# A transformer layer on eight cores: a reordered head, evened head pairs, and wider rows of values

## The chip, the cores and the metric

The kernel runs on the eight cores of one Trainium2 chip. Each core takes one of the eight sequences of the batch and works alone; all cores hold a copy of the weights. The metric is the device time in microseconds of the slowest core.

## The reference

For one sequence x of 2048 rows and 1024 columns:

```
xn  = layernorm(x)
q, k, v = xn Wq, xn Wk, xn Wv            (16 heads of 64 columns)
out = softmax(q k^T / 8) v               (per head)
x1  = x + xn + out Wp
h   = layernorm(x1) W1 W2 W3             (three 1024 x 1024 weights)
y   = x1 + tanh(h + bias)
```

The kernel folds W1 W2 W3 into one matrix on the chip (the "folds"), since nothing nonlinear stands between them.

## The kernel before

There are five engines with a queue of instructions each: TensorE (matmuls and transposes), ScalarE, VectorE, GpSimd and SyncE. All waits are written out by hand: `need(engine, token)` makes an engine wait for a semaphore, and an engine works through its instructions in the order in which the Python code emits them. Where a function is called therefore decides what stands behind what.

**The head** (lines 555 to 677). The 16 tiles of x, 128 rows each, are loaded by SyncE (L172). For each tile VectorE makes the statistics (`ln1_stats`: bn_stats L559, bn_aggr L561) and adds epsilon (L567), GpSimd raises to the power -1/2 (L569) and forms minus mean times that (`nm`, L575). The normalised tile `xn` is written by GpSimd (L579), every fourth by ScalarE (`ln1_se`, L584). Tiles 0 and 1 go singly; from tile 2 on, `ln1_power` serves two tiles at once, so that it waits for the statistics of both. TensorE transposes each tile in eight pieces (`ln1_turn`, L604), and ScalarE copies the result into `S` (L610). Once four tiles are in `S`, a group g of 512 rows can be projected: `first_proj` runs eight matmuls of 512 columns for q or k (`proj_mms`, L217) or 32 of 128 columns for v (`v_mms`, L256). Weight slices of one head pair are loaded by GpSimd's queue (`load_slice`, L178), each with a cast from float to bfloat16 (512 KB read, 256 KB written); the first, wk of pair 0, is issued before the memsets that fill both buffers of v with ones (L187). In the loop of L619, group g's k and q projections follow the transposes of its own tiles, and its v projection stands before the transposes of the next group's last two tiles. After the loop come k and q of group 3, two k groups of pair 1 (`unit_k`, L646 and L658), the squares of q and k (`square`, L234, on VectorE), and the guard: three small steps (`guard1` to `guard3`, L289, L302, L311) that turn the largest squared norms into one constant `cb`, which every exponential of the pair subtracts. `guard1` needs all squares of q and k. Between the guards TensorE does half of v's last group.

**The loop** (L760) goes over 8 pairs of heads, in each over 8 chunks of 256 query rows, and in each over 8 units of two key tiles. `emit_qk` makes scores for both heads (L370), `emit_exp` one exponential of 128 x 1024 (L382), `emit_pv` eight matmuls (L398): the probabilities are the weights, and 65 columns of v are the moving operand: 64 values of one head of one key tile and a column of ones, which gives the row sum. Such a row of v lies in SBUF at a stride of VW = 66 elements of 2 bytes, 132 bytes. The results of a chunk stand in one PSUM bank, again at a stride of 66 (there of 4 bytes). `emit_norm` divides by the sums, `turn_ao` transposes.

Between these, TensorE has filler units: projections of the next pair (`unit_k`, `unit_q`, `unit_v`), and the folds (`unit_w12`, `unit_w123`), 32 in all, spread over pairs 0 to 6 by `N_FOLD`. `queue_pair` lists the units of a pair. A chunk has two regular places for a unit; what a pair has over 16 (`extra`) is put in by an additional `advance(8)` and `finish()` in chunk 1 or 3, after step 1. The listed units before are 16 in pairs 0 to 4 and 6, and 17 in pair 5. All of them share one PSUM bank, so that a unit starts only when the eviction of the one before, by VectorE, is done. The last fold of W1 W2 starts the load of W3, and it stands first in pair 3.

**The tail** adds x1, the output projection, the second normalisation and the folded matrix, row tile by row tile.

Of the kernel before, what the change touches and what calls it, by code (L numbers as in the profile page):

```python
# [9 lines left out]
F32 = mybir.dt.float32  # L10
# [7 lines left out]
NT = N // 128  # L18
NK = D // 128
NP = 8  # L20
EPS = 1e-5
VW = 66

QC = 256
NSLOT = 3
# [26 lines left out]
def build_program():  # L52
# [14 lines left out]
    with ctx:  # L67
        def sb(name, cols, dt):
            return E(nc.sbuf_tensor(name, [128, cols], dt))
# [17 lines left out]
        onesb = sb("onesb", 1, BF16)  # L87
        sixteenth = sb("sixteenth", 128, F32)
        biasb = sb("biasb", D, F32)
        mhalf = sb("mhalf", 2, F32)  # L90
        st6 = [sb(f"st6_{i}", 12, F32) for i in range(4)]
        mv = sb("mv", 2 * NT, F32)
        ve = sb("ve", NT, F32)
        rs = sb("rs", NT, F32)
        rs1 = sb("rs1", NT, F32)
        nm = sb("nm", NT, F32)
        mv2 = sb("mv2", 2 * NT, F32)
        ve2 = sb("ve2", NT, F32)
        rs2 = sb("rs2", NT, F32)
# [77 lines left out]
        def load_slice(n, p):  # L177
            return d_w[n][p % 2].inc(GP.dma_start(wsl[n][p % 2][:], wqkv_d[n, p]))  # L178

        w_in = {(1, 0): load_slice(1, 0)}  # L180
        half_in = s_gp.inc(GP.memset(mhalf[:], -0.5))
        need(SE, half_in)
        s_se.inc(SE.activation(nm2[:, 0:1], mhalf[:, 0:1], AF.Identity))
# [202 lines left out]
        def emit_pv(t):  # L386
            p, c, u = iters[t]
            need(TE, exp_in[t])
            if u == 0:
                need(TE, bank_free[PV0])  # L390
            for i in range(MPI):
                m = MPI * u + i
                need(TE, v_in[(p, m // 4)])
                for qt in range(NQT):
                    for h in range(2):
                        col = VW * (qt * 2 + h)
                        off = 512 * h + QC * i + 128 * qt
                        ins = TE.matmul(bank[PV0][:, col:col + 65],  # L398
                                        P[t % NPB][:, off:off + 128],
                                        v[p % 2][:, VW * (2 * m + h):VW * (2 * m + h) + 65],  # L400
                                        start=(u == 0 and i == 0 and qt == 0 and h == 0),
                                        stop=(u == NU - 1 and i == MPI - 1), skip_group_check=True)
            pv_mm[t] = s_te.inc(ins)
            pv_done[p] = pv_mm[t]

        def emit_norm(p, c):

            i = (p * NCQ + c) % 2
            nb = 2 * NQT
            need(VE, pv_done[p], norm_in.get((p * NCQ + c) - 2))  # L410
            sums = bank[PV0][:, 0:VW * nb].rearrange("p (g c) -> p g c", c=VW)
            m = s_ve.inc(VE.reciprocal(rc[i][:], sums[:, :, 64]))
            need(VE, m, ao_mm.get((p * NCQ + c) - 2))
            norm_in[p * NCQ + c] = bank_free[PV0] = s_ve.inc(VE.tensor_tensor(  # L414
                ao[i][:].rearrange("p (g c) -> p g c", c=64), sums[:, :, 0:64],
                rc[i][:].unsqueeze(2).to_broadcast([128, nb, 64]), ALU.mult))
# [135 lines left out]

        xn1 = [xn[i] if i < NXN else P[i - NXN] for i in range(2 * NXN)]

        def ln1_stats(t):
            need(VE, x_in[t])
            st = st6[t % 4]
            for h in range(2):
                m = s_ve.inc(VE.bn_stats(st[:, 6 * h:6 * (h + 1)], x_tile[t][:, 512 * h:512 * (h + 1)]))  # L559
            need(VE, m)  # L560
            return s_ve.inc(VE.bn_aggr(mv[:, 2 * t:2 * t + 2], st[:]))  # L561

        def ln1_power(t, n, m):

            var = mv[:, 2 * t:2 * (t + n)].rearrange("p (t c) -> p t c", c=2)[:, :, 1]
            need(VE, m)
            m = s_ve.inc(VE.tensor_scalar(ve[:, t:t + n], var, EPS, None, ALU.add))  # L567
            need(GP, m, gp_ones)
            m = s_gp.inc(GP.tensor_tensor(rs[:, t:t + n], ve[:, t:t + n], mhalf[:, 0:n], ALU.pow))  # L569
            need(GP, m)  # L570

        nm_in = {}

        def ln1_gp(t):
            nm_in[t] = m = s_gp.inc(GP.tensor_scalar(nm[:, t:t + 1], mv[:, 2 * t:2 * t + 1], rs[:, t:t + 1],  # L575
                                                     -1.0, ALU.mult, ALU.mult))
            if t % 4 != 0:
                need(GP, m, t1_mm.get(t - 2 * NXN))
                xn_in[t] = s_gp.inc(GP.tensor_scalar(xn1[t % (2 * NXN)][:], x_tile[t], rs[:, t:t + 1],  # L579
                                                     nm[:, t:t + 1], ALU.mult, ALU.add))  # L580
# [6 lines left out]
        def ln1_pair(j):

            if j == 0:
                ln1_power(0, 1, ln1_stats(0))  # L590
                ln1_gp(0)
                ln1_power(1, 1, ln1_stats(1))
                ln1_gp(1)
                return
            ln1_stats(2 * j)
            ln1_power(2 * j, 2, ln1_stats(2 * j + 1))
            ln1_gp(2 * j)
            ln1_gp(2 * j + 1)

        def ln1_turn(t, eng, sem):  # L600
            b = next_bank()
# [8 lines left out]
            bank_free[b] = sem.inc(SE.copy(dst, src) if eng is SE else VE.tensor_copy(dst, src))  # L610
            S_in[t // 4].append(bank_free[b])

        def first_proj(n, g):

            b = next_bank()
            run(v_mms(0, g, b) if n == 2 else proj_mms(n, 0, g, b))
            return b

        for j in range(NT // 2 + 1):  # L619
            g = j // 2 - 1  # L620
            if j < NT // 2:
                ln1_pair(j)
            if j == 0:
                w_in[(0, 0)] = load_slice(0, 0)
            if j == 1:
                w_in[(2, 0)] = load_slice(2, 0)
            if j == 5:
                w_in[(1, 1)] = load_slice(1, 1)
            if j % 2 and g >= 0:
                evict_qk(0, 0, g, held[0], SE, s_se)  # L630
            if j > 0:
                ln1_turn(2 * j - 2, SE, s_se)
                last = (VE, s_ve) if 2 * j == NT else (SE, s_se)
                ln1_turn(2 * j - 1, *last)
            if j < NT // 2 and j % 2 == 0:
                ln1_se(2 * j)
            if g >= 0 and j < NT // 2:
                if j % 2 == 0:
                    held = {1: first_proj(1, g), 0: first_proj(0, g)}
                    evict_qk(1, 0, g, held[1], SE, s_se)  # L640
                else:
                    held[2] = first_proj(2, g)
                    evict_v(0, g, held[2], SE, s_se)


        run(unit_k(1, 0, squared=False))  # L646
        b = first_proj(1, 3)
        evict_qk(1, 0, 3, b, VE, s_ve)
        for g in range(3):
            square(1, 0, g)  # L650
            square(0, 0, g)
        square(1, 0, 3)
        b = first_proj(0, 3)
        evict_qk(0, 0, 3, b, SE, s_se)
        square(0, 0, 3)
        ring["banks"] = [4, 5, 6, 7]
        ring["i"] = 0
        run(unit_k(1, 1, squared=False))  # L658
        guard1(0, next_bank())()
        for t in range(BATCH):  # L660
            emit_qk(t)
        guard2(0, next_bank())()
        b = next_bank()
        values = v_mms(0, 3, b)
        for _ in range(16):
            next(values)
        guard3(0, next_bank())()
        run(values)
        evict_v(0, 3, b, VE, s_ve)
        for g in range(2):  # L670
            square(1, 1, g)
        need(GP, x_in[NT - 1])
        for n in (0, 2):
# [4 lines left out]

        need(VE, xn_in[NT - 2], xn_in[NT - 1])
        rs1_in = s_ve.inc(VE.tensor_scalar(rs1[:], rs[:], 1.0, None, ALU.add))
        ring["banks"] = [FL0]

# [188 lines left out]
```

How the kernel before makes its waits and increments, by code:

```python
    def inc(self, instr):  # L46
        instr.then_inc(self.h, self.step)
        self.n += self.step
        return (self, self.n)
# [2 lines left out]
def build_program():  # L52
# [106 lines left out]
        def need(eng, *tokens):  # L159
            for tok in tokens:
                if tok is None:
                    continue
                sem, n = tok
                if waited.get((eng, sem), 0) < n:
                    eng.wait_ge(sem.h, n)
                    waited[(eng, sem)] = n
# [652 lines left out]
        turn_ao(NP - 1, NCQ - 1, next_bank())()  # L820
        push_chunk(NCQ - 1)
        for t, fh in ((NT - 3, 0), (NT - 3, 1), (NT - 2, 0)):
            units.append(unit_ff(t, fh))
        units.append(unit_t2(NT - 1))
        for t, fh in ((NT - 2, 1), (NT - 1, 0), (NT - 1, 1)):
            units.append(unit_ff(t, fh))
        while units:
            run(units.popleft())
        for s in d_o:
            SP.wait_ge(s.h, s.n)
        nc.all_engine_barrier()
    return nc
```

## Time and profile before

| | us |
|---|---|
| median of 3 runs | 728.6 |
| lowest, highest | 728.41, 823.76 |
| profiled execution | 729.96 |
| its span, core 6 (the slowest) | 728.2 |
| spans of the other cores | 725.1 to 727.6 |
| TensorE, ScalarE, VectorE, GpSimd busy | 681.6, 599.4, 264.4, 125.3 |

The span is the time from the first to the last instruction of a core; the profiled execution's own time is a little longer. An engine's busy time counts the time in which at least one of its instructions was at work. Matmuls overlap in the pipeline, so a single one lasts longer in the records than the distance to the next; the chain of waits gives runs of matmuls by that distance. The highest of the three runs is far above the other two; the median is not moved by it.

### The profile page before, as it was taken

How to read it: one execution, taken by the hardware profiler on the slowest of the kernel's cores; microseconds unless marked ns; L12 is line 12 of the kernel's file. 1: busy time of each engine (PE TensorE's matmuls, PEld its weight loads, DVE VectorE, ACT ScalarE, POOL GpSimd, SP SyncE). 2: the span in 40 equal slices, each digit the busy share in tenths (PEclk: the TensorE clock that was granted, in tenths of full speed). 3: DMA queues.
4: the chain of work that ended last, by engine and by line, in shares of the span. 5: the costliest groups of instructions: out<-in, count | busy, mean ns of one | idle time of the engine just before them, and what ended most of it. 6: DMA issues, size and time to landing. Idle time of an engine off the chain costs nothing.

```text
span 728.2 us, 21958 instructions; the slowest of 8 cores (725.1 to 728.2 us)
## 1 busy us (share of the span) xinstructions
PE 681.6 (94%) x9112; PEld 432.3 (59%) x9112; DVE 264.4 (36%) x590; ACT 599.4 (82%) x600; POOL 125.3 (17%) x169
## 2 busy tenths in 40 slices
PE   1699999999999999999999999999999989999996
PEld 0465676667666765676667656665676555444443
DVE  4724322332223322322332233224322343556663
ACT  2566999999999999999999989999999899444443
POOL 5871000000000002000000000012010121366654
PEclk9999999999999999999999999999999999999999
DMA  8959700111010004610110000032024000334332
GB/s 229 283 72 166 135 9 3 16 16 16 4 16 2 2 3 69 107 17 2 17 22 12 16 2 3 2 88 88 2 41 80 1 3 2 109 124 155 134 116 116
DMA packets 13344, 41.87 MB, mean 57 GB/s; under 512 B 1600, under 2 KB 1728, under 8 KB 13248
## 3 DMA queue, kind: packets, MB, share of 16 engines
q0 software_dynamic: 5904, 15.21, 13.7%
q1 hardware_dynamic: 7056, 25.17, 10.4%
q8 instruction: 74, 1.21, 0.7%
q14 instruction: 22, 0.18, 0.1%
q10 hardware_dynamic: 288, 0.10, 0.1%
HBM read 46.76 MB, written 8.39 MB: 76 GB/s over the span
## 4 chain that ended last, share of the span: by engine, by line
PE 86%; DVE 4%; issue 3%; DMA 3%; ACT 3%; POOL 0%; DVEq 0%; SPq 0%; ACTq 0%; POOLq 0%
PE sc L370 18%; PE pv L398 16%; PE fl L217 14%; PE fl L256 8%; PE sc L521 5%; PE fl L343 4%; PE fl L326 4%; PE sc L464 4%; PE fl L464 3%; ACT P L382 2%; DMA aoT<-x 2%; PE fl L422 2%; PE sc L217 1%; DMA wv<-wqkv 1%; PE pv L521 1%
## 5 line engine op out<-in xcount | busy, mean ns | idle before, releaser
L382 ACT ACTIVATE P<-sc,cb 128x1024 bf16<-128x1024 f32 x512 | 528.3, 1114 | 36.4 <-PE sc L370 24.4
L398 PEld LDWEIGHTS pv<-v,P 128*128 128x128 bf16 x4096 | 157.7, 97 | 44.1 <-issue 17.2
L398 PE MATMUL pv<-v,P 128*128 128x65 bf16 x4096 | 173.5, 193 | 5.4 <-DVE ao L414 2.6
L370 PE MATMUL sc<-qT,kT 64*128 64x256 bf16 x2048 | 157.5, 272 | 1.8 <-ACT P L382 1.8
L370 PEld LDWEIGHTS sc<-qT,kT 64*128 64x128 bf16 x2048 | 78.5, 94 | 42.8 <-issue 25.2
L532 ACT ACTIVATE S<-S 128x512 f32<-128x512 f32 x32 | 20.1, 629 | 58.2 <-DVE S L528 58.2
L256 PE MATMUL fl<-wv,S 128*128 128x128 bf16 x960 | 63.6, 219 | 1.8 <-DVE aoT L429 0.4
L256 PEld LDWEIGHTS fl<-wv,S 128*128 128x128 bf16 x960 | 54.1, 98 | 12.4 <-issue 12.2
L217 PE MATMUL fl<-S,wq 128*128 128x512 bf16 x224 | 57.8, 380 | 0.5
L217 PE MATMUL fl<-S,wk 128*128 128x512 bf16 x208 | 53.5, 380 | 3.1 <-DVE ao L414 1.3
L268 DVE CAST v<-fl 128x512 bf16<-128x512 f32 x29 | 20.0, 691 | 78.8 <-PE fl L256 78.8
L521 PE MATMUL sc<-bufB,S 128*128 128x512 bf16 x192 | 45.0, 379 | 0.5 <-ACT S L514 0.5
L540 POOL TENSOR_TENSOR S<-S,xs 128x512 f32<-128x512 f32 x30 | 38.1, 1271 | 41.8 <-ACT S L532 41.8
L228 DVE CAST qT<-fl 128x512 bf16<-128x512 f32 x28 | 19.4, 691 | 71.1 <-PE fl L217 71.1
L228 DVE CAST kT<-fl 128x512 bf16<-128x512 f32 x26 | 18.0, 691 | 67.6 <-PE fl L217 67.6
L326 PE MATMUL fl<-bufA,bufB 128*128 128x512 bf16 x128 | 33.1, 380 | 1.1 <-DVE g L306 0.7
L343 PE MATMUL fl<-bufA,bufC 128*128 128x512 bf16 x128 | 33.1, 380 | 1.0 <-DVE g L306 0.8
L457 POOL TENSOR_SCALAR xs<-xs,rs,nm 128x1024 f32<-128x1024 f32 x16 | 19.2, 1202 | 75.1 <-DVE aoT L429 72.6
L464 PE MATMUL sc<-bufC,aoT 128*128 128x512 bf16 x136 | 32.1, 379 | 0.0
L521 PEld LDWEIGHTS sc<-bufB,S 128*128 128x128 bf16 x192 | 18.6, 98 | 22.6 <-issue 0.9
L217 PEld LDWEIGHTS fl<-S,wq 128*128 128x128 bf16 x224 | 17.5, 97 | 24.0 <-issue 9.8
L429 DVE COPY aoT<-fl 128x256 bf16<-128x256 bf16 x63 | 18.3, 291 | 35.7 <-PE fl L422 13.4
(128 smaller groups left out, 555.8 us busy)
## 6 DMA issues: line engine op xcount, KB each, us to landing
xs<-x SPq DMA_DIRECT2D x22, 512.0 KB, 6.0
out<-S SPq DMA_DIRECT2D x15, 512.0 KB, 2.9
aoT<-x SPq DMA_DIRECT2D x8, 512.0 KB, 12.7
wk<-wqkv POOLq DMA_DIRECT2D x8, 256.0 KB, 9.0
wq<-wqkv POOLq DMA_DIRECT2D x8, 256.0 KB, 4.9
wv<-wqkv POOLq DMA_DIRECT2D x8, 256.0 KB, 5.9
bufA<-w1t POOLq DMA_DIRECT2D x4, 512.0 KB, 14.3
bufB<-w POOLq DMA_DIRECT2D x4, 512.0 KB, 25.0
```

Source lines behind the costliest of these rows:

```text
L217: ins = TE.matmul(bank[b], wsl_k[n][p % 2][:, k, :], S_k[:, k, 512 * g:512 * (g + 1)], start=(k == 0), stop=(k == NK - 1))
L228: SE.copy(dst, bank[b]) if eng is SE else VE.tensor_copy(dst, bank[b]))
L256: ins = TE.matmul(bank[b][:, 128 * j:128 * (j + 1)], S_k[:, k, 128 * t:128 * (t + 1)], wsl_k[2][p % 2][:, k, :], start=(k == 0), stop=(k = ...
L326: ins = TE.matmul(bank[b], B_k[:, k, 128 * e:128 * (e + 1)], A_k[:, k, 512 * ch:512 * (ch + 1)], start=(k == 0), stop=(k == NK - 1))
L343: ins = TE.matmul(bank[b], C_k[:, k, 128 * ct:128 * (ct + 1)], A_k[:, k, 512 * fh:512 * (fh + 1)], start=(k == 0), stop=(k == NK - 1))
L370: ins = TE.matmul(sc[s][:, 512 * h + QC * i:512 * h + QC * (i + 1)], kT[p % 2][64 * h:64 * (h + 1), 128 * m:128 * (m + 1)], qT[p % 2][64 * ...
L382: exp_in[t] = s_se.inc(SE.activation(P[t % NPB][:], sc[s][:], AF.Exp, bias=cb[p % 2][:], scale=0.125))
L398: ins = TE.matmul(bank[PV0][:, col:col + 65], P[t % NPB][:, off:off + 128], v[p % 2][:, VW * (2 * m + h):VW * (2 * m + h) + 65], start=(u ...
L464: ins = TE.matmul(bank[b], ao_k[:, k, 128 * t:128 * (t + 1)], C_k[:, k, 512 * fh:512 * (fh + 1)], start=(k == 0), stop=(k == NK - 1))
L521: ins = TE.matmul(bank[b], xn2T[t % 3][:, k, :], B_k[:, k, 512 * fh:512 * (fh + 1)], start=(k == 0), stop=(k == NK - 1))
L532: m = s_se.inc(SE.activation(h, h, AF.Tanh))
L540: add_done[t] = s_gp.inc(GP.tensor_add(h, h, x1_tile(t)[:, 512 * fh:512 * (fh + 1)]))
```

## The change

1. The stride of a row of v goes from 66 to 96 elements (132 to 192 bytes). The stride in PSUM stays 66, now called PW. The two buffers of v grow from 4,224 to 6,144 bytes a partition each.
2. The head: each tile of x goes through its own statistics and power; VectorE also writes the negated mean (`ngm`), and GpSimd normalises as (x + ngm) x rs in one instruction, so that it needs no `nm` first. Only every fourth tile makes `nm` at once; VectorE makes the whole `nm` later, for the tail. Tile 15 is normalised by VectorE. wk of pair 0 is loaded when x0 is in. v of a group is projected after the transposes of the next group's tiles (g = 0) or among them. Three k groups of pair 1 are now projected in the head, the first two inside the loop over groups. Six of the eight squares move into the loop over groups. Eight v matmuls, not sixteen, stand between the second and third guard, and eight before the first.
3. `N_FOLD` goes from [7, 4, 4, 4, 4, 5, 4] to [8, 4, 4, 4, 4, 4, 4], and no fold is moved to the front of pair 3. Pair 0 lists one k projection fewer. Each of pairs 0 to 6 then lists 16 units.

```diff
-VW = 66
+VW = 96
+PW = 66
...
-        w_in = {(1, 0): load_slice(1, 0)}
+        w_in = {}
...
-                        col = VW * (qt * 2 + h)
+                        col = PW * (qt * 2 + h)
...
-            sums = bank[PV0][:, 0:VW * nb].rearrange("p (g c) -> p g c", c=VW)
+            sums = bank[PV0][:, 0:PW * nb].rearrange("p (g c) -> p g c", c=PW)
...
-        def ln1_stats(t):
+        def ln1_tile(t):
...
+            m = s_ve.inc(VE.bn_aggr(mv[:, 2 * t:2 * t + 2], st[:]))
             need(VE, m)
-            m = s_ve.inc(VE.tensor_scalar(ve[:, t:t + n], var, EPS, None, ALU.add))
+            s_ve.inc(VE.tensor_scalar(ngm[:, t:t + 1], mv[:, 2 * t:2 * t + 1], -1.0, None, ALU.mult))
+            m = s_ve.inc(VE.tensor_scalar(ve[:, t:t + 1], mv[:, 2 * t + 1:2 * t + 2], EPS, None, ALU.add))
             need(GP, m, gp_ones)
-            m = s_gp.inc(GP.tensor_tensor(rs[:, t:t + n], ve[:, t:t + n], mhalf[:, 0:n], ALU.pow))
-            need(GP, m)
+            m = s_gp.inc(GP.tensor_tensor(rs[:, t:t + 1], ve[:, t:t + 1], mhalf[:, 0:1], ALU.pow))
+            if t % 4 == 0:
+                need(GP, m)
+                nm_in[t] = s_gp.inc(GP.tensor_tensor(nm[:, t:t + 1], ngm[:, t:t + 1], rs[:, t:t + 1], ALU.mult))
+                return
+            eng, sem = (VE, s_ve) if t == NT - 1 else (GP, s_gp)
+            need(eng, m, t1_mm.get(t - 2 * NXN))
+            xn_in[t] = sem.inc(eng.tensor_scalar(xn1[t % (2 * NXN)][:], x_tile[t], ngm[:, t:t + 1],
+                                                 rs[:, t:t + 1], ALU.add, ALU.mult))
...
+        need(GP, x_in[0])
+        w_in[(1, 0)] = load_slice(1, 0)
+        for t in range(4):
+            ln1_tile(t)
+            if t == 0:
+                ln1_se(0)
+            if t == 1:
+                w_in[(0, 0)] = load_slice(0, 0)
+            ln1_turn(t, SE, s_se)
+        w_in[(2, 0)] = load_slice(2, 0)
+        for g in range(NT // 4 - 1):
+            t0 = 4 * g + 4
+            ln1_tile(t0)
+            ln1_tile(t0 + 1)
+            ln1_se(t0)
+            bk = first_proj(1, 0, g)
+            bq = first_proj(0, 0, g)
+            evict_qk(1, 0, g, bk, SE, s_se)
+            ln1_turn(t0, SE, s_se)
+            evict_qk(0, 0, g, bq, SE, s_se)
+            ln1_turn(t0 + 1, SE, s_se)
+            ln1_tile(t0 + 2)
+            ln1_tile(t0 + 3)
+            if g == 0:
                 w_in[(1, 1)] = load_slice(1, 1)
+                ln1_turn(6, SE, s_se)
+                ln1_turn(7, SE, s_se)
+                evict_v(0, 0, first_proj(2, 0, 0), SE, s_se)
+            elif g == 1:
+                bv = first_proj(2, 0, 1)
+                ln1_turn(10, SE, s_se)
+                evict_v(0, 1, bv, SE, s_se)
+                ln1_turn(11, SE, s_se)
+                evict_qk(1, 1, 0, first_proj(1, 1, 0), SE, s_se)
+            else:
+                for h in range(3):
+                    square(1, 0, h)
+                    square(0, 0, h)
+                ln1_turn(14, SE, s_se)
+                bv = first_proj(2, 0, 2)
+                ln1_turn(15, VE, s_ve)
+                evict_v(0, 2, bv, SE, s_se)
+                evict_qk(1, 1, 1, first_proj(1, 1, 1), SE, s_se)
+        b = first_proj(1, 0, 3)
         evict_qk(1, 0, 3, b, VE, s_ve)
-        for g in range(3):
-            square(1, 0, g)
-            square(0, 0, g)
         square(1, 0, 3)
-        b = first_proj(0, 3)
+        b = first_proj(0, 0, 3)
         evict_qk(0, 0, 3, b, SE, s_se)
         square(0, 0, 3)
-        ring["banks"] = [4, 5, 6, 7]
+        evict_qk(1, 1, 2, first_proj(1, 1, 2), SE, s_se)
+        ring["banks"] = [7, 4, 5, 6]
         ring["i"] = 0
-        run(unit_k(1, 1, squared=False))
+        b = next_bank()
+        values = v_mms(0, 3, b)
+        for _ in range(8):
+            next(values)
         guard1(0, next_bank())()
...
-        need(VE, xn_in[NT - 2], xn_in[NT - 1])
+        need(VE, xn_in[NT - 4], xn_in[NT - 2])
+        s_ve.inc(VE.tensor_mul(nm[:], ngm[:], rs[:]))
...
-        N_FOLD = [7, 4, 4, 4, 4, 5, 4]
+        N_FOLD = [8, 4, 4, 4, 4, 4, 4]
...
-            if p == 3:
-                units.append(mine.pop(0)())
-            for g in range(2 if p == 0 else 0, 4):
+            for g in range(3 if p == 0 else 0, 4):
```

## Rows read from the trace of the kernel before

**Rows 1.** The page: busy time by engine, and the chain's shares.

```profile
PE 681.6 (94%) x9112; PEld 432.3 (59%) x9112; DVE 264.4 (36%) x590; ACT 599.4 (82%) x600; POOL 125.3 (17%) x169
...
PE 86%; DVE 4%; issue 3%; DMA 3%; ACT 3%; POOL 0%; DVEq 0%; SPq 0%; ACTq 0%; POOLq 0%
```

**Rows 2.** Busy time by window, from first exponential to first exponential: pairs 4, 5.

```profile
core 6: us, PE busy (x) PEld busy (x) DVE busy (x) ACT busy (x) POOL busy (x), PEclk, DMA share, GB/s
...
340.45:409.65 69.20, 68.48 (x1045) 45.73 (x1043) 21.26 (x51) 66.13 (x64) 1.58 (x3) 1.00 0.09 13
409.65:481.58 71.93, 70.42 (x1053) 46.47 (x1051) 21.95 (x52) 66.20 (x64) 0.53 (x1) 1.00 0.03 6
```

**Rows 3.** The same for chunk 1 of pair 4 and of pair 5.

```profile
348.94:357.34 8.40, 8.40 (x118) 5.03 (x114) 3.04 (x7) 8.24 (x8) 0.00 (x0) 1.00 0.06 11
...
418.23:429.41 11.18, 10.30 (x126) 5.72 (x122) 4.15 (x9) 8.37 (x8) 0.00 (x0) 1.00 0.01 3
```

**Rows 4.** Chain of waits, 418 to 430 us: start, length, what.

```profile
424.33 1.90 PE fl L217 x8
...
426.32 0.70 DVE kT L228
```

**Rows 5.** Timeline, 0 to 40 us: start, length, instruction, idle before, releaser.

```profile
1.56 0.75 POOL L178 DMA_DIRECT2D wk<-wqkv  x1 [0.88 <-POOLq L53]
...
2.51 3.68 POOL L187 MEMSET v<- 128x2112 bf16 x2
...
8.82 0.15 DVE L567 TENSOR_SCALAR ve<-mv 128x1 f32<-128x1 f32 x1
...
9.19 0.57 POOL L569 TENSOR_TENSOR rs<-ve,mhalf 128x1 f32<-128x1 f32 x1 [3.00 <-DVE ve L567]
...
15.08 1.28 DVE L559 BATCH_NORM_STATS2 st<-aoT 128x6 f32<-128x512 f32 x2 [0.40 <-DMA aoT<-x]
16.46 0.21 DVE L561 BATCH_NORM_AGGREGATE mv<-st 128x2 f32<-128x12 f32 x1
...
17.11 0.72 POOL L569 TENSOR_TENSOR rs<-ve,mhalf 128x2 f32<-128x2 f32 x1 [3.28 <-DVE ve L567]
...
20.04 1.19 POOL L579 TENSOR_SCALAR xn<-aoT,rs,nm 128x1024 bf16<-128x1024 f32 x1 [0.18 <-POOL nm L575]
...
23.64 3.57 PE L217 MATMUL sc<-S,wk 128*128 128x512 bf16 x8 [1.25 <-ACT S L610]
...
30.47 1.95 PE L256 MATMUL sc<-wv,S 128*128 128x128 bf16 x32 [0.51 <-DMA wv<-wqkv]
...
35.07 1.89 PE L217 MATMUL sc<-S,wk 128*128 128x512 bf16 x8 [1.76 <-ACT S L610]
```

**Rows 6.** DMA issues up to 25 us: KB each, us from issue to landing.

```profile
wk<-wqkv POOLq DMA_DIRECT2D x1, 256.0 KB, 11.2
wq<-wqkv POOLq DMA_DIRECT2D x1, 256.0 KB, 8.9
wv<-wqkv POOLq DMA_DIRECT2D x1, 256.0 KB, 9.2
```

**Rows 7.** Timeline, 39 to 63 us.

```profile
39.26 1.02 ACT L610 COPY S<-sc 128x1024 bf16<-128x1024 bf16 x1
...
44.02 1.89 PE L217 MATMUL sc<-S,wk 128*128 128x512 bf16 x8 [1.76 <-ACT S L610]
...
46.00 0.58 ACT L228 CAST kT<-sc 128x512 bf16<-128x512 f32 x1 [0.99 <-PE sc L217]
```

**Rows 8.** Chain of waits, 54 to 62 us.

```profile
55.71 1.41 DVE sq L234 x4
...
61.52 1.12 ACT P L382
```

**Rows 9.** Chain of waits, 28 to 120 and 340 to 350 us: runs of matmuls.

```profile
39.58 1.80 PE fl L256 x32
...
81.66 0.53 PE pv L398 x16
...
343.76 0.50 PE pv L398 x16
...
345.58 0.50 PE pv L398 x16
```

More of the change, by code:

```diff
@@ L89, in build_program @@
         biasb = sb("biasb", D, F32)
-        mhalf = sb("mhalf", 2, F32)
+        mhalf = sb("mhalf", 1, F32)
         st6 = [sb(f"st6_{i}", 12, F32) for i in range(4)]
@@ L96, in build_program @@
         nm = sb("nm", NT, F32)
+        ngm = sb("ngm", NT, F32)
         mv2 = sb("mv2", 2 * NT, F32)
@@ L560, in ln1_stats @@
             need(VE, m)
-            return s_ve.inc(VE.bn_aggr(mv[:, 2 * t:2 * t + 2], st[:]))
-        def ln1_power(t, n, m):
-            var = mv[:, 2 * t:2 * (t + n)].rearrange("p (t c) -> p t c", c=2)[:, :, 1]
+            m = s_ve.inc(VE.bn_aggr(mv[:, 2 * t:2 * t + 2], st[:]))
             need(VE, m)
-            m = s_ve.inc(VE.tensor_scalar(ve[:, t:t + n], var, EPS, None, ALU.add))
+            s_ve.inc(VE.tensor_scalar(ngm[:, t:t + 1], mv[:, 2 * t:2 * t + 1], -1.0, None, ALU.mult))
+            m = s_ve.inc(VE.tensor_scalar(ve[:, t:t + 1], mv[:, 2 * t + 1:2 * t + 2], EPS, None, ALU.add))
             need(GP, m, gp_ones)
-            m = s_gp.inc(GP.tensor_tensor(rs[:, t:t + n], ve[:, t:t + n], mhalf[:, 0:n], ALU.pow))
-            need(GP, m)
-        nm_in = {}
[L574 to L580, printed above, removed]
+            m = s_gp.inc(GP.tensor_tensor(rs[:, t:t + 1], ve[:, t:t + 1], mhalf[:, 0:1], ALU.pow))
[7 more added lines that the diff above has]
+                                                 rs[:, t:t + 1], ALU.add, ALU.mult))
+        nm_in = {}
         def ln1_se(t):
@@ L585, in ln1_se @@
                                               bias=nm[:, t:t + 1], scale=rs[:, t:t + 1]))
[L587 to L598, printed above, removed]
         def ln1_turn(t, eng, sem):
@@ L611, in ln1_turn, with first_proj @@
             S_in[t // 4].append(bank_free[b])
-        def first_proj(n, g):
+        def first_proj(n, p, g):
             b = next_bank()
-            run(v_mms(0, g, b) if n == 2 else proj_mms(n, 0, g, b))
+            run(v_mms(p, g, b) if n == 2 else proj_mms(n, p, g, b))
             return b
[L619 to L623, printed above, removed]
-                w_in[(0, 0)] = load_slice(0, 0)
-            if j == 1:
-                w_in[(2, 0)] = load_slice(2, 0)
-            if j == 5:
-                w_in[(1, 1)] = load_slice(1, 1)
[L629 to L643, printed above, removed]
@@ L646, in build_program @@
-        run(unit_k(1, 0, squared=False))
-        b = first_proj(1, 3)
+        need(GP, x_in[0])
[5 more added lines that the diff above has]
+            if t == 1:
+                w_in[(0, 0)] = load_slice(0, 0)
+            ln1_turn(t, SE, s_se)
[14 more added lines that the diff above has]
+            if g == 0:
+                w_in[(1, 1)] = load_slice(1, 1)
+                ln1_turn(6, SE, s_se)
[16 more added lines that the diff above has]
+                evict_qk(1, 1, 1, first_proj(1, 1, 1), SE, s_se)
@@ L662, in build_program @@
         guard2(0, next_bank())()
-        b = next_bank()
-        values = v_mms(0, 3, b)
-        for _ in range(16):
+        for _ in range(8):
             next(values)
@@ L669, in build_program @@
         evict_v(0, 3, b, VE, s_ve)
-        for g in range(2):
+        for g in range(3):
             square(1, 1, g)
```

## The prediction

> **What bounds the kernel now.** I read the times first: the profiled execution took 729.96 us, 1.4 above the median of the runs (728.6), and core 6, the slowest, has a span of 728.2. Then the page: TensorE is busy for 94% of the span and has 86% of the chain that ended last; ScalarE is busy for 82% [rows 1]. Then the span cut at the first exponential of each head pair: a pair takes 69.2 us when nothing unusual is in it, and TensorE is busy for 68.5 of them, ScalarE for 66.1 [rows 2]. A chunk of eight exponentials takes 8.40 us, with TensorE busy for all 8.40 [rows 3]. So a nanosecond taken from TensorE inside the loop shortens it, as long as a chunk stays above the 8.24 us for which ScalarE is busy in it. The part before the first exponential, at 61.52 us, is a chain through all engines: x tiles landing, statistics on VectorE, power and normalisation on GpSimd, transposes on TensorE, copies on ScalarE [rows 5, 7, 8].
>
> **Part 1, pair 5 loses its odd unit.** Each pair's gaps are filled with projection and fold units. Two per chunk fit into the regular places. Before, pair 5 has 17 for 8 chunks, and the 17th gets a place of its own in chunk 1. That chunk takes 11.18 us where the same chunk of pair 4 takes 8.40 [rows 3]; the chain there shows the unit's eight matmuls (1.90) and an eviction that TensorE waits for (0.70) [rows 4]. The whole of pair 5 is 71.93 against 69.20 for pair 4 [rows 2]. After, pairs 0 to 6 have 16 each. Pair 0 swaps one k projection, now done in the head, for a fold; both are eight matmuls of 512 columns and one eviction, so pair 0 costs the same. The fold that pair 3 did first is now the last of pair 2's, so the load of w3 starts earlier. Gain: 11.18 - 8.40 = 2.8; by whole pairs 2.7. I take **2.7**, ends 2.5 and 2.8.
>
> **Part 2, the head up to the first k projection.** Before, it starts at 23.64 and waits for tile 3: tiles 2 and 3 share one power, which waits for the statistics of both (17.11, 0.72); the normalisations of tiles 2 and 3 follow it on GpSimd, the last from 20.04 for 1.19, to 21.23 [rows 5]. After, each tile has its own power (0.57 as for tile 0), and tile 2's normalisation no longer waits for tile 3. If x3 still lands just before 15.08, VectorE gives its variance at 15.08 + 1.28 + 0.21 + two small operations of 0.15 with their gaps = 17.1; power 0.57, gap 0.2, normalisation 1.19: 19.1 instead of 21.23, a gain of 2.1. Also, wk's load is now issued only when x0 is in. It was issued at 1.56, so it shares the DMA engines with x1 to x3, and VectorE waits for x3 until 15.08 [rows 5]. A slice reads 0.5 MB, one x tile's worth, and by VectorE's pace in these rows a tile comes every 2 us. Moved behind x0, that traffic may fall after x3: up to 2 us more, but then the power and normalisation of two tiles in turn on GpSimd (2 us each) bind, so 1.4. I take 3.1 in all, ends 1.5 and 3.7. What is moved past what: GpSimd's queue now holds the memsets of v, then the wait for x0, then wk. The memsets grow with the row, 3.68 x 96/66 = 5.35, from 2.51 to 7.9, so wk is issued at 7.9. Landing takes 11.2 us for the first wk, 8.9 to 9.2 for wq and wv [rows 6]: 17 to 19, just ahead of a first projection at 20.5. wq (issued near 13) lands by 22, needed at 24; wv (near 19) by 28, needed at 28. This cover is thin: if wk comes later than 20.5, the head pays the difference. SyncE's queue of x tiles is not touched.
>
> **Part 3, from there to the first exponential.** Before it takes 23.64 to 61.52 = 37.9. In it TensorE waits for wv and for copies before the second and third k projections: 0.51 before 30.47, 1.76 before 35.07 and 1.76 before 44.02, 4.0 together [rows 5, 7]. Behind the last evictions eight squares stand in a row on VectorE, four of them 1.41 [rows 8]; the guard needs them. After, v of group g comes after the transposes of g+1, and the new projections of pair 1 sit in front of the third and last groups, so that the copies have cover. Along ScalarE's order (a copy is 1.02, a cast 0.58 [rows 7]) I still find stalls of 0.4 to 1.7 and 0.6, so I count 2.0 where 4.0 were. Added: one k projection more, 1.73, and 8 of 16 v matmuls moved ahead of the guard (no net cost; 0.3 less between the second and third guard, since the reduction covers them). Six squares move to where VectorE has nothing to do. Sum: -4.0 + 2.0 + 1.7 - 0.3 = -0.6, and -1.0 with the wait for the squares, some 0.4. Some of this will be lost to what arrives late: x12 to x15 now share the DMA engines with wk for pair 1, issued earlier, and each tile costs VectorE 0.15 us more for the negated mean. I take **-0.2 for part 3**, ends -1.1 and +0.7. Parts 2 and 3 together: 3.1 + 0.2 = **3.3** gained, ends 0.8 and 4.8; first exponential at 58.2. TensorE runs at 1.2 GHz for the first ten or so big matmuls (3.57 us for eight, against 1.89 later, the pace of 2.4 GHz), though the granted clock reads 1.00 [rows 5]; nothing here changes how many.
>
> **Part 4, the rows of v.** 4,096 matmuls of 65 columns read a row of 130 bytes. It began at multiples of 132; now at multiples of 192. A run of 16 takes 0.50 to 0.53 us [rows 9], 31.4 ns each. For comparison, a matmul of 128 columns whose rows begin at multiples of 256 bytes takes 1.80/32 = 56.2 ns, 2.9 above its 53.3 at 2.4 GHz; by this 65 columns are 27.1 + 2.9 = 30.0. So the excess that alignment could remove is 1.4 ns x 4,096 = 5.7 us; even at the full speed of 27.1 it could not be above 17.6. Against a gain: a row that begins at 132j begins 0, 4, ... 60 bytes into a 64-byte unit, and 60 + 130 = 190 < 192, so every row touches three units before and three after. Runs alternate between rows whose starts lie 0 to 28 bytes into a unit (343.76) and 32 to 60 (345.58); both take 0.50 [rows 9]. A loss of the same size is not excluded: the rows of both heads now begin at the same place of a unit, and the nearest price is the spread of the runs, 0.53 against 0.50, or 0.03 x 256 = 7.7 us. I take **0**, ends 7.7 lost and 9 gained (the excess, and the spread of its reading on top). Evictions into v read 512 floats of PSUM either way: 0.
>
> The Trainium skill, "SBUF — State Buffer", Specifications, speaks of 16-byte cachelines and a penalty at each cross to a new one. A row of 130 bytes starting 0, 4, 8 or 12 bytes into such a line touches nine lines in each case, so by that rule nothing would be gained, and the trace neither shows nor denies it.
>
> **Sum.** 2.7 + 3.3 = 6.0. The profiled execution would go from 729.96 to 724.0, the median from 728.6 to **722.6**.
>
> **Rivals.**
> A. Head and pairs gain, v's rows do nothing: 722.6, by the bounds of parts 1 to 3 (3.3 to 7.6 gained) 721.0 to 725.3. 56%.
> B. Aligned rows take the excess away from each value matmul: 728.6 - 6.0 - 5.7 = 716.9, and 713.5 with the 9 us. TensorE bounds the chunks (8.40 against 8.24 for ScalarE [rows 3]), and 5.7 us over 64 chunks are 0.09 each, so they pass through. For: the excess is there. Against: both kinds of runs cost the same. 29%. The Trainium skill, "TensorE: Matmul & The Clock Gate", Back-to-back issue gap, gives N/2.4 + 2.5 ns, by which 65 columns take 29.6; the estimate from the page is that 1.8 ns x 4,096 = 7.4 us of excess exist, 715.2 if alignment removes it all. The trace's 56.2 for 128 columns agrees with the same formula.
> C. Slower: the new rows make the value matmul (line 400) slower. At the 7.7 us of the spread: 728.6 - 6.0 + 7.7 = 730.3. It decides from 1.5 ns a matmul on, where it outweighs the 6.0. Nothing in the rows speaks for it but that a row's place can matter at all. 7%.
> D. The head gives nothing, because the late wk holds the first projection or stalls return in other places; pair 5 alone: 725.9, or 727 with a loss of 1. 8%.
>
> **Numbers.** Range: A, D and most of B: 714 to 727, which leaves out C and that end of B. Faster by over 2% (about what a measurement of this kernel can tell from no change) means under 714.0: only B's far end, 10%. Slower by over 2%, above 743.2, would need 5 ns more for each value matmul: 1%. Within: 89%.
>
> **What the profile after will show.** Part 1: pair 5 as long as pair 4, no 11 us chunk. Part 2: the first k projection near 20.5, no wait for wk. Part 3: first exponential near 58.2, no row of six squares ahead of the guard. Part 4: runs of 16 value matmuls still at 0.50; at 0.47 or less B is right, above 0.53 C. If pairs 1 to 4 change length at all, it is v's rows, since nothing else in them is touched.

## The result

The changed kernel takes 722.34 us in the median of its runs, the kernel before 728.89 beside it: 0.9915 of it, 95% interval 0.9895 to 0.9935, so 6.2 us faster. The forecast was 722.6. The ratio, and the figures over all runs below, leave out executions in which one die's cores ran at a lower granted clock (one of the five of after, at 740.24 us). The profiled execution of after has spans of 716.1 to 720.2 us over the cores (core 4 the longest); before they went from 725.1 to 728.2.

Core 4 of the kernel after, busy time by window, pairs 4 and 5, chunk 1 of pair 4, and pair 3 (columns: window, length, then PE, PEld, DVE, ACT, POOL busy, granted clock, DMA share, GB/s). They answer to [rows 2, 3]:

```profile
335.30:404.32 69.02, 68.27 (x1045) 45.36 (x1043) 21.36 (x51) 66.08 (x64) 1.59 (x3) 1.00 0.10 14
404.32:473.32 69.00, 68.28 (x1045) 45.38 (x1043) 21.37 (x51) 66.13 (x64) 0.53 (x1) 1.00 0.04 6
264.08:335.30 71.22, 68.57 (x1045) 45.68 (x1043) 21.36 (x51) 66.29 (x64) 4.77 (x9) 1.00 0.33 50
...
412.77:421.13 8.36, 8.36 (x118) 4.99 (x114) 3.05 (x7) 8.23 (x8) 0.00 (x0) 1.00 0.06 11
```

Pair 5 is now as long as pair 4, and both are a little shorter than before (69.20). But pair 3, 69.2 on most cores before, is 71.2 here. The head, in the timeline of the same core, answers to [rows 5]:

```profile
1.27 5.25 POOL L189 MEMSET v<- 128x3072 bf16 x2
...
6.46 0.77 POOL L180 DMA_DIRECT2D wk<-wqkv  x1
...
12.76 1.29 DVE L562 BATCH_NORM_STATS2 st<-aoT 128x6 f32<-128x512 f32 x2 [0.94 <-DMA aoT<-x]
...
15.56 1.20 POOL L576 TENSOR_SCALAR xn<-aoT,ngm,rs 128x1024 bf16<-128x1024 f32 x1 [0.18 <-POOL rs L569]
...
19.16 3.57 PE L219 MATMUL sc<-S,wk 128*128 128x512 bf16 x8 [1.25 <-ACT S L596]
...
30.57 1.89 PE L219 MATMUL sc<-S,wk 128*128 128x512 bf16 x8 [1.36 <-ACT S L596]
...
39.97 1.89 PE L219 MATMUL sc<-S,wk 128*128 128x512 bf16 x8 [0.48 <-ACT S L596]
```

x3 is there at 12.76 instead of 15.08, the first k projection starts at 19.16 instead of 23.64, and TensorE's stalls after it are 1.36 + 0.48 = 1.8 us instead of 4.0. The chain of waits just before the first exponential answers to [rows 8]; no square stands in it any more:

```profile
47.15 6.91 PE sc L219 x32
54.06 0.45 PE fl L258 x8
54.51 0.78 PE sc L291 x32
...
57.27 1.12 ACT P L384
```

The runs of value matmuls, two of them in the chain of after:

```profile
430.70 0.49 PE pv L400 x16
...
434.86 0.49 PE pv L400 x16
```

and their group on its page (the first number behind the bar is the busy time in us; before it was 173.5):

```profile
L400 PE MATMUL pv<-v,P 128*128 128x65 bf16 x4096 | 170.7, 193 | 6.9 <-DVE ao L416 2.6
```

A table by stage says where the time went. Each figure is the median over the eight cores of one profiled execution, from first exponential to first exponential (pair 7 to its last exponential, "rest" from there to the end of the span); "run" is the time from the first to the last start in 16 value matmuls. The columns e1 to e10 are experiments told below.

| us | before | after | e1 | e2 | e3 | e9 | e10 |
|---|---|---|---|---|---|---|---|
| first exponential | 61.24 | 56.41 | 56.24 | 60.60 | 61.97 | 55.44 | 56.61 |
| pair 0 | 69.52 | 68.80 | 69.97 | 69.04 | 69.53 | 69.00 | 69.09 |
| pair 1 | 69.56 | 68.89 | 69.21 | 69.21 | 69.29 | 68.89 | 68.90 |
| pair 2 | 69.19 | 69.24 | 69.54 | 68.89 | 69.19 | 69.25 | 69.25 |
| pair 3 | 69.20 | 69.75 | 69.88 | 69.07 | 69.93 | 68.86 | 68.89 |
| pair 4 | 69.19 | 69.02 | 69.31 | 68.89 | 69.19 | 69.01 | 69.03 |
| pair 5 | 71.89 | 69.01 | 69.31 | 71.55 | 69.20 | 71.55 | 69.01 |
| pair 6 | 69.53 | 69.13 | 69.59 | 69.13 | 69.50 | 69.26 | 69.09 |
| pair 7 | 70.26 | 70.78 | 71.01 | 70.45 | 70.95 | 70.32 | 69.72 |
| rest | 106.74 | 106.81 | 106.84 | 106.72 | 106.73 | 106.77 | 106.94 |
| span | 727.0 | 718.4 | 721.8 | 724.1 | 725.8 | 719.3 | 716.4 |
| run, ns | 472 | 455 | 472 | 455 | 472 | 455 | 455 |

One profile is one sample. The profiled execution of before is a long one: its median core has 727.0 us, over all runs it has 725.7 to 726.0; for after the two agree (718.4). So the median core gained 7.4 us and not 8.6.

The time that counts is that of the slowest core, and the slowest core is further from the median one in some kernels than in others. The reason turned out to be part of the answer.

### The profile page after: what moved, and what is told of

Read it like the earlier page. It is cut to its first block, busy times and chain, and to the rows that moved or that the text cites. A ratio compares the mean times of both kernels' runs of the same rounds, so it can differ in the third digit from the quotient of the medians.

```text
span 720.2 us, 21977 instructions; the slowest of 8 cores (716.1 to 720.2 us)
## 1 busy us (share of the span) xinstructions
PE 679.9 (94%) x9112; PEld 429.9 (60%) x9112; DVE 264.8 (37%) x612; ACT 600.8 (83%) x603; POOL 125.3 (17%) x163
## 3 DMA queue, kind: packets, MB, share of 16 engines
q8 instruction: 74, 1.21, 0.7%
## 4 chain that ended last, share of the span: by engine, by line
PE 88%; ACT 3%; DVE 3%; issue 3%; DMA 1%; POOL 0%; SPq 0%; DVEq 0%; ACTq 0%; POOLq 0%
PE sc L372 18%; PE pv L400 16%; PE fl L219 14%; PE fl L258 8%; PE sc L523 5%; PE fl L345 4%; PE fl L328 4%; PE sc L466 4%; PE fl L466 3%; PE sc L219 3%; ACT P L384 2%; PE fl L424 2%; DMA aoT<-x 1%; PE pv L523 1%; PE fl L291 1%
## 5 line engine op out<-in xcount | busy, mean ns | idle before, releaser
L400 PEld LDWEIGHTS pv<-v,P 128*128 128x128 bf16 x4096 | 155.0, 97 | 47.3 <-issue 20.0
L400 PE MATMUL pv<-v,P 128*128 128x65 bf16 x4096 | 170.7, 193 | 6.9 <-DVE ao L416 2.6
L258 PEld LDWEIGHTS fl<-wv,S 128*128 128x128 bf16 x960 | 54.1, 98 | 12.1 <-issue 11.6
L219 PE MATMUL fl<-S,wk 128*128 128x512 bf16 x200 | 51.7, 381 | 1.0 <-DVE aoT L431 0.2
L180 POOL DMA_DIRECT2D wv<-wqkv x8 | 4.4, 547 | 161.6 <-PE pv L400 156.5
## 6 DMA issues: line engine op xcount, KB each, us to landing
bufA<-w1t POOLq DMA_DIRECT2D x4, 512.0 KB, 12.6
```

The lines of the kernel that those rows point to most:

```text
L219: ins = TE.matmul(bank[b], wsl_k[n][p % 2][:, k, :], S_k[:, k, 512 * g:512 * (g + 1)], start=(k == 0), stop=(k == NK - 1))
L258: ins = TE.matmul(bank[b][:, 128 * j:128 * (j + 1)], S_k[:, k, 128 * t:128 * (t + 1)], wsl_k[2][p % 2][:, k, :], start=(k == 0), stop=(k = ...
L400: ins = TE.matmul(bank[PV0][:, col:col + 65], P[t % NPB][:, off:off + 128], v[p % 2][:, VW * (2 * m + h):VW * (2 * m + h) + 65], start=(u ...
```

## The experiments

**e1, new head and pairs, old rows.**

```diff
-VW = 96
+VW = 66
```

> The changed kernel with the rows of v back at 132 bytes. Theory 1 (the head and the evened pairs carry nearly all, the rows a little): a run of 16 value matmuls goes back from 455 to about 472 ns between the first and the last start, pair 4 from 69.02 to 69.20 us, and the time is 722.3 + 8 x 0.2 = 724 us. Theory 2 (the rows do nothing for the time): 722.3, within 0.5. Theory 3 (every ns that TensorE saves on value matmuls, 17 ns x 256 runs = 4.4 us, reaches the end): 726.7.

Measured: 726.17 us, 0.9957 of before (0.9944 to 0.9971). The run is 472 ns, pair 4 69.31. So the rows of 192 bytes are worth 3.8 us in time with this head (3.1 by the two ratios to before). The median core's span says 3.4: 0.3 us in each of pairs 1, 2, 4 and 5, and more in pairs 0 and 6. This also leaves 3.1 us for everything else in the change: 729.34 before beside it, 726.17 here. Theory 1 had the rows at 0.2 a pair and came out too low; theory 3's 726.7 is nearest in time. With the same rows, pair 2 is 0.35 and pair 4 0.12 longer here than in the kernel before; no run says why.

**e2, the old head with new rows.**

```diff
-VW = 66
+VW = 96
+PW = 66
```

> The kernel before with the rows of v at 192 bytes alone, PSUM stride kept at 66. Theory 1: pair 4 at 69.02 instead of 69.20, time 728.9 - 1.5 = 727.4 us; first exponential unchanged near 61.2 (the longer memset of v, 5.3 instead of 3.7 us, ends before x0's statistics need GpSimd). Theory 2: 728.9. Theory 3: 724.5.

Measured: 728.85, 0.9995 (0.9986 to 1.0003). Here too the run is 455 ns, and pairs 1, 2 and 4 are shorter by 0.30 to 0.35; the median core gains 1.6 us over all runs (725.7 to 724.1). The time gains 0.5, which its interval does not tell from nothing. What the slowest core lost in this program is seen in its trace: a gap of 2.1 us at 541 us on core 5, the slowest. The spread of the slowest core is only part of the difference between e1 and e2: on the median core too the rows are worth 3.4 us in e1 and 1.6 here. Where the other 1.8 lie stays open.

**e3, the old head with evened pairs.**

```diff
         run(unit_k(1, 1, squared=False))
+        run(unit_k(1, 2, squared=False))
...
-        N_FOLD = [7, 4, 4, 4, 4, 5, 4]
+        N_FOLD = [8, 4, 4, 4, 4, 4, 4]
...
-            if p == 3:
-                units.append(mine.pop(0)())
-            for g in range(2 if p == 0 else 0, 4):
+            for g in range(3 if p == 0 else 0, 4):
```

> The kernel before with the pairs evened alone: a third k group of pair 1 is projected in the old head, behind the second, pair 0 has 8 folds, pair 5 loses its 17th unit. Theory (pair 5's extra place costs 2.8 us, and in the old head the unit has no cover): first exponential 0.5 to 1.7 us later, since the squares (2.2 us on VectorE) already cover part of the 1.73 us; pair 5 at 69.2 instead of 71.9; time 728.9 - 2.7 + 1.0 = 727.2 us. Rival (the extra place is filled by something else, so that evening is worth nothing by itself): 728.9 to 730.6.

Measured: 731.15, 1.0023 (1.0013 to 1.0033): slower by 1.7 us. Pair 5 does lose its 2.7 us. But the head gives back 0.7, pair 3 0.7 and pair 7 0.7. Neither theory had this: the gain is there and is given back in the head and in pairs that did not get more units. These parts come from one profile, of the fastest of e3's executions (728.04). Over all of them the median core is where it was (725.7 before, 725.8 here), and the slowest core is later.

**e4, rows of 144 bytes**: `VW = 72` in the kernel after.

> The changed kernel with rows of v of 144 bytes: each begins at a multiple of 16 bytes, not of 64. Theory a (only the place in 16 bytes matters): the same 455 ns for a run of 16 and 722.3 us as with 192. Theory b (64 bytes matter, as the change's words say): the run lies between 455 and 472 ns and the time up to 1.7 us above. Theory c (a conflict between places in the address that repeat with the stride): the run may be below 455, since 144 spreads the starts over four places in 64 bytes.

Measured: 721.82, 0.9909 (0.9891 to 0.9926), run 455 ns, pair 4 at 68.99. Multiples of 16 bytes do all that multiples of 64 do, in 3 KB less of each partition.

**e12, rows of 136 bytes**: `VW = 68`.

> The changed kernel with rows of v of 136 bytes, multiples of 8 bytes and not of 16; one look at the pace only. Theory a (16 bytes decide): a run of 16 value matmuls takes 470 to 472 ns between the first and last start, as with 132. Theory b (8 bytes are enough): 455. Theory c (the share of rows that begin at a multiple of 16 decides, here half, with 132 a quarter): about 464.

Measured: 465 ns, pair 4 at 69.17, one run of 724.1 us. In the recorded starts, a matmul whose row begins 8 bytes past a multiple of 16 is followed after 33 ns, one whose row begins at a multiple after 29; from the third matmul of a run on the medians alternate strictly, 29, 33, 29, 33. The first two distances are 29 and 35 with every stride. With 132 bytes a quarter of the rows begins at a multiple of 16, and 9 of the 15 distances of a run are 32 to 35; with 192 there are no 33s left, but two or three 35s. Theory c came within 1 ns. Its rule is not the whole of it: with 132 bytes two rows that begin 8 bytes past a multiple of 16 (the seventh and the fifteenth of a run) are followed after 29 ns all the same, and no run says why.

**e7, results 512 bytes apart in PSUM**: `PW = 128` in the kernel after.

> The changed kernel with the stride of the results in PSUM at 128 elements (512 bytes) instead of 66 (264 bytes). Theory a (what is left above 29.2 ns between two value matmuls, some intervals of 35, comes from where the results begin): a run goes from 455 to 438 to 445 ns, time 722.3 - 1 to 2. Theory b (it comes from elsewhere): 455 ns and 722.3 us. VectorE's reads of the results are of the same size either way.

Measured: 722.38, 0.9913 (0.9880 to 0.9947), run 455 ns. Between these two strides, where the results begin plays no part; the 35s stay unexplained.

**e6, wk first again.**

```diff
-        w_in = {}
+        w_in = {(1, 0): load_slice(1, 0)}
...
-        need(GP, x_in[0])
-        w_in[(1, 0)] = load_slice(1, 0)
```

> The changed kernel with wk of pair 0 issued first again, before the memsets, as in the kernel before. Theory (the late wk gives x1 to x3 the DMA engines, 1.0 us of the head's gain, the rest comes from the single tiles and the order): first k projection 1 us later than 19.2, first exponential at 57.4 instead of 56.4 (median of the cores), time 723.3 us. Rival a (the DMA engines' share does not matter, as the same bytes move before x3): no change, 722.3. Rival b (nearly all of the gain before the first projection, 4.5 us, is the late wk): 725.5.

Measured: 724.41, 0.9931 (0.9913 to 0.9948). Over the cores' medians VectorE starts on x3 at 14.3 instead of 12.6, the first k projection starts at 20.7 instead of 19.2, and the first exponential comes at 58.3 instead of 56.4. Of the 3.9 us that the change gains before the first projection (23.0 to 19.2), the late wk is 1.6 in these profiles, and 2.3 are left for the single tiles. The other profiles show how far to trust that: the same old head has its first projection at 22.4 to 22.5 in e2, e3 and e8, and the new one at 19.0 to 19.5 in all runs with a late wk. So the gain is 2.9 to 4.0, the late wk 1.2 to 1.7 of it. In time e6 lies 1.2 us above after by the ratios, and their intervals overlap.

**e9, the new head with the old pairs.** The third k group of pair 1 leaves the head, and `N_FOLD` and pair 3 are as before.

> The changed kernel (new head, rows of 192 bytes) with the pairs as before: 17 units in pair 5, two k groups of pair 1 in the head, w3's load at the start of pair 3. Theory (evening gains 2.7 us in pair 5 and gives back the k group's 1.1 to 1.7 us in the head and up to 0.7 in pair 3): first exponential at 54.7 to 55.5 instead of 56.4 (median of the cores), pair 5 at 71.6, pair 3 at 69.1 to 69.4, time 722.3 to 723.5 us. Rival (the evening is worth its 2.7 us on the new head, where the k group is covered): 725.0.

Measured: 723.22, 0.9930 (0.9906 to 0.9953), against 0.9915 (0.9895 to 0.9935) with evened pairs: the two are not told apart. The table has the parts: evening takes 2.5 from pair 5, gives 1.0 back in the head, 0.9 in pair 3 and 0.5 in pair 7.

**What pair 3 loses.** In the chain of waits of after (core 4), chunk 1 of pair 3:

```profile
273.62 0.30 PE pv L400 x10
273.92 1.29 issue
275.21 0.34 PE pv L400 x6
```

TensorE stops for 1.29 us in the middle of 16 matmuls whose operands have long been there, and waits for nothing that the profile shows. The window of that chunk, with the DMA share second from the right:

```profile
272.53:282.29 9.76, 8.47 (x118) 5.11 (x114) 3.13 (x7) 8.34 (x8) 0.00 (x0) 1.00 1.03 147
```

The DMA engines are full: w3's four parts, issued from 265.67 us on by the last unit listed for pair 2, and the three slices of chunk 1. Over all cores of the first six profiles, every gap above 0.8 us inside a run of value matmuls lies at 70 to 81, 273 to 281 or 539 to 551 us, that is beside the loads of w1t and w2, of w3, and of wp. The page's DMA part has a queue "instruction":

```profile
q8 instruction: 74, 1.21, 0.7%
```

These are 74 packets of 16 KB, 1.21 MB over the span, about one in 8 us. By the queue's name they bring an engine's instructions, and they travel on the same DMA engines as the loads. The next experiments ask whether the loads are the cause.

**e10, no loads of w3 and wp.**

```diff
-                fold["w3_in"] = load_big(bufA, d_A, "w3", [fold["w12_mm"]])
+                fold["w3_in"] = A_in
...
-                fold["wp_in"] = load_big(bufC, d_C, "wp", [fold["w123_mm"]])
+                fold["wp_in"] = [fold["w12_in"]]
```

> The changed kernel without the loads of w3 and wp; the folds and the output projection read what lies in their buffers, so this output is not the reference's, and all instructions on the engines are the same. Theory (the gaps at 273 to 275 and 540 to 550 us come from these loads, which fill the DMA engines while TensorE's next instructions have to be fetched): no gap above 0.7 us there on any core, pair 3 from 69.75 to 69.0, pair 7 from 70.8 to 70.2, and the slowest core nearer to the median one: time 722.3 - 1.5 to 2.5 = 720.3. Rival (the gaps belong to the program, not to the loads): unchanged, 722.3.

Measured: 719.00, 0.9858 (0.9836 to 0.9880). No core has a gap above 0.7 us near 273 or 540. Pair 3 on core 4:

```profile
263.06:331.94 68.88, 68.15 (x1045) 45.37 (x1043) 21.26 (x51) 66.03 (x64) 1.58 (x3) 1.00 0.09 14
```

The spans lie between 715.7 and 717.2 us, 1.5 apart where after has 4.1. So the two loads cost 3.3 us in time (4.2 by the ratios to before), and 1.9 on the median core over all runs; the rest falls on the core that happens to be the slowest. The theory holds.

What TensorE waits for in these stops can be read from the packets of the queue "instruction". Over all fourteen profiles and all cores, between 62 and 600 us, there are 121 distances above 0.8 us between the starts of two neighbouring matmuls of one group. Every one of them ends 0.8 to 1.6 us (median 1.4) after a packet of this queue has landed, and it is always one of the same seven packets of the 74: number 4, 5, 29, 30, 34, 61 or 62. In the kernel after, packet 29 is the one of pair 3. On the four cores that stop there it starts 12.6 to 13.6 us after packet 28, and TensorE goes on 1.3 to 1.5 us after it has landed. On the other four cores it starts 11.6 to 11.8 us after packet 28 and has landed 2.0 to 2.2 us before the same matmul: no stop. Without the loads (e10) it starts 8.5 us after packet 28 on every core and has landed over 5 us before that matmul. So the loads delay the packet by 3 to 5 us, and TensorE stands where the next packet of its program has not come in time.

**e5, w3 cut in time.**

```diff
-                fold["w3_in"] = load_big(bufA, d_A, "w3", [fold["w12_mm"]])
+                fold["w3_in"] = []
...
+            if p == 3 and c in (2, 3, 4, 5) and step == 0:
+                need(GP, fold["w12_mm"], pv_mm[t0 - 1])
+                i = c - 2
+                fold["w3_in"].append(d_A[i].inc(GP.dma_start(bufA[:, 2048 * i:2048 * (i + 1)],
+                                                             big_d["w3"][:, 2048 * i:2048 * (i + 1)])))
```

> The changed kernel with the load of w3 cut in time: its four parts are issued one per chunk in chunks 2 to 5 of pair 3, behind the slices of chunk 1, instead of all at once at the end of pair 2. Theory (the load, on full DMA engines together with the three slices, holds back TensorE's instructions: gaps of 0.9 to 1.5 us inside a run of value matmuls at 273 to 275 us): those gaps go, pair 3 goes from a median of 69.75 us over the cores (69.3 to 71.2) to 69.1 to 69.3, and the time from 722.3 to about 721.3. Rival (pair 3 is long because of its own order of units): pair 3 stays at 69.7 and the time at 722.3.

Measured: 724.98, 0.9941 (0.9926 to 0.9957): 2.6 us above the 722.3 of after (1.9 by the ratios, whose intervals just overlap), and the median core is 1.2 us later over all runs. On the median core pair 3 is at 69.1 as the theory says, but core 6 has 70.4 and core 7 74.0 there, beside the last of the four parts (315 and 316 us).

**e8, the same on the old head with evened pairs.**

> The kernel before with evened pairs (as in e3_old_head_even_pairs, 731.15 us) and w3's load cut in time as in e5_paced_w3. Theory (evening's gain of 2.7 us in pair 5 was lost to 0.7 us in the head, and to gaps beside the loads of w3 and wp, 0.7 us each at the median and more on the slowest core): pair 3 back from 69.9 to 69.2, time 730.2. Rival (the evening loses elsewhere): 731.1.

Measured: 732.86, 1.0047 (1.0032 to 1.0063). Both theories were wrong: pair 3 is 72.4 in the median and 74.7 on core 0. Here is what happens to core 0 beside the last part, first in the windows:

```profile
316.00:320.00 4.00, 4.00 (x93) 3.42 (x90) 0.69 (x1) 3.85 (x5) 0.99 (x2) 1.00 0.59 86
320.00:324.00 4.00, 0.99 (x31) 0.87 (x28) 0.39 (x2) 1.68 (x2) 0.00 (x0) 0.75 0.98 164
324.00:328.00 4.00, 4.00 (x43) 3.27 (x41) 0.00 (x0) 1.15 (x2) 0.00 (x0) 0.50 0.11 20
328.00:332.00 4.00, 3.99 (x61) 2.99 (x60) 1.20 (x3) 3.06 (x3) 0.00 (x0) 0.90 0.00 0
```

and in the chain of waits:

```profile
320.49 0.12 PE pv L398 x3
320.60 3.01 issue
323.61 0.90 PE pv L398 x13
324.51 1.71 PE fl L256 x16
326.21 0.97 PE sc L370 x8
327.18 1.80 PE fl L256 x16
328.99 0.50 PE pv L398 x16
```

TensorE stands for 3.0 us. The granted clock falls to 0.50, its lower level of 1.2 GHz, within the stop (the 0.75 is the mean of that window), and stays there for about 7 us: eight score matmuls take 0.97 instead of 0.54, sixteen of v 1.71 to 1.80 instead of 0.9 to 1.05. Gap and slow stretch together cost this pair 5.5 us. The DMA engines were full for a few us only. Cutting a load does not make it harmless; it makes four places out of one at which it can meet a moment when TensorE runs dry, and on this program the last of them is met by seven cores of eight, always at packet 34. The clock does not fall after every stop: it did after twelve of the 121, which lasted 1.3 to 3.6 us, and did not after others of 2.0 to 3.3. e9's core 0 shows the same beside wp's load:

```profile
542.49 0.21 PE pv L400 x7
542.70 1.76 issue
544.46 0.53 PE pv L400 x9
544.99 0.84 PE sc L372 x8
```

**e11, slices of pairs 0 and 3 later.**

```diff
-            if (c, step) == (1, 0) and p + 2 < NP:
+            if (c, step) == (4 if p in (0, 3) else 1, 0) and p + 2 < NP:
```

> The changed kernel with the three weight slices of pairs 0 and 3 issued in chunk 4 instead of chunk 1, so that they no longer follow directly on the large loads (w1t, w2 and the bias in pair 0, w3 in pair 3). Theory (a shorter time of full DMA engines around 70 to 80 and 273 to 290 us catches fewer of the fetches): pairs 0 and 3 shorter by 0 to 0.7 us on the median core, 721.5 to 722.3 us. Rival (as with w3 cut in time, the new place hits a fetch that was free before): above 722.5.

Measured: 722.70, 0.9913 (0.9892 to 0.9934): no change. Pair 3 is 69.60 where after has 69.75. The large load alone is enough.

## Why the prediction was right, and where it was not

The sign was right, and the time to 0.3 us, but that closeness is luck. Head and pairs together were to give 6.0 us and the rows nothing. Measured, the change without its rows gave 3.1 (e1 against before), and the rows 3.1 to 3.8 more. The two errors cancel. Rival A, the one that the forecast rests on, was wrong on the rows.

**Part 1 (evened pairs, 2.7 gained) failed as a net term.** The step itself held: pair 5 lost 2.9 us, of which 0.3 are the rows. What failed is the step that lets the load of w3 start earlier and gives this no price. With evened pairs, pair 3 is 0.9 us longer on the median core (69.75 against 68.86 in e9, with the same rows; 0.55 against before, whose rows are the old ones), 2.0 longer than before on core 4, and pair 7 is 0.5 longer. That pair 3 pays for w3's load is shown by e10. Why pair 7 pays, where wp's load did not move, stays open. On the old head evening made the kernel 1.7 us slower (e3); on the new one it is worth 0.9 us by the medians, within the intervals (e9). The k group in the head, which I priced with the head, costs 1.0 there.

**Part 2 (3.1 gained, ends 1.5 and 3.7) was right in kind.** Measured 3.9 in the two profiles' medians of the cores, 2.9 to 4.0 over all profiles of the two heads (e6). The late wk gave 1.6 of it (1.2 to 1.7), where I had 1.0 because I let GpSimd's pace bind; for the single tiles I had 2.1, and 2.3 are left. wk never held anything up, as said. Its issue was at 6.46, not 7.9: with the wk load gone from the front, the memsets start 1.2 us earlier.

**Part 3 (0.2 gained)** came out at 61.24 - 23.02 = 38.2 before and 56.41 - 19.15 = 37.3 after, 0.9 gained, near the far end of 1.1 (0.4 to 1.0 with the other profiles of the new head). The stalls are 1.8, where I counted 2.0, and the squares are off the chain. Parts 2 and 3 were forecast at 3.3 and measure 4.8 in these two profiles; the first exponential lies at 60.6 in e2, which has the old head too, and at 56.2 to 57.3 over the runs that have the whole new head, so 3.4 to 5.0.

**Part 4 (rows, 0) was wrong**, and rival B, at 29%, was half right: the mechanism is real (455 ns for 472, 1.1 ns for each matmul, 4.4 us of TensorE), and 3.4 us of it reach the median core with the new head, 1.6 with the old one. Even in a plain chunk not all of it arrives: 17 ns for each of its four runs are 0.07 us, and the chunk went from 8.40 to 8.36. My argument against it counted units of 64 bytes, before and after three, and saw no difference between runs whose rows begin in different halves of a unit. It missed the place within 16 bytes, because every run of 16 holds all four places, so that no run could show it. The Trainium skill's 16-byte cachelines ("SBUF — State Buffer", Specifications) were the right size. Counting the lines touched, nine in every case, as I did beside it, misses the cost: e12 shows that the start matters where the number of lines does not change. The Trainium skill's formula for an isolated matmul, N/2.4 + 2.5 ns or 29.6 ns for 65 columns ("TensorE: Matmul & The Clock Gate", Back-to-back issue gap), agrees with the 29 ns of the rows that begin at a multiple of 16.

The chances do not fit the range either. It leaves out rival C (7%) and B's far end (10%), which makes 83% within, not 89%; and B's far end adds up to 713.6, not 713.5.

In sum, by the medians of the cores in the two profiles: gained are 4.8 in the head, 2.9 in pair 5, 0.7 each in pairs 0 and 1, 0.4 in pair 6 and 0.2 in pair 4; given back are 0.55 in pair 3, 0.5 in pair 7 and 0.1 elsewhere. That makes 8.5, of 8.6 between the median spans of the two profiles, and 7.4 over all runs. The time fell by only 6.2 to 6.6, because it is the slowest core's, and the slowest core is the one with the stops.

## What to carry to other kernels

A load that no instruction waits for is not free: while it fills the DMA engines, the packets that bring TensorE's instructions can come too late, and a TensorE that stands for over a microsecond may come back at half its clock; look for "issue" gaps in the middle of runs, on every core, and compare spreads between cores and not only medians. A small moving operand that is read thousands of times should begin at a multiple of 16 bytes; here 144 bytes a row instead of 132 do it. And check an argument of alignment at every power of two, since a view that averages over all places shows none of them.

## What the runs showed of the hardware

- A matmul of 65 columns whose moving row begins off a multiple of 16 bytes is followed 3 to 4 ns later (33 for 29) than one whose row begins on it; 136-byte rows show it one by one, 144 and 192 are equal. With 132 bytes, two of the twelve rows of a run that begin off it are not followed later.
- The place of its results in PSUM (264 or 512 bytes apart) changes nothing.
- Stops of 0.8 us and more inside a run of value matmuls came only beside loads from GpSimd's queue, and not on all cores; beside w3 and wp they were gone without those loads.
- All 121 stops ended 0.8 to 1.6 us after a 16 KB packet of the queue "instruction" had landed, always one of the same seven of 74; full DMA engines brought packet 29 up to 5 us later than idle ones (8.5 us after the one before it in e10, 11.6 to 13.6 in after).
- After twelve stops of 1.3 to 3.6 us the granted clock was at 0.50 for 3 to 7 us, and after others of up to 3.3 us it was not. On core 0 of e8 stop and slow stretch cost 5.5 us together, of which the stop is 3.0.
